# Sixteen pad writes issued before, not after, the placement of the last attention maxima

## The reference

```python
xn = layernorm(x)
x = x + L0_attn(xn) + L0_ffn(xn)
xn = layernorm(x)
x = x + L1_attn(xn) + L1_ffn(xn)

# L1_ffn, for xt of shape (T, 128)
topk_logits, topk_idx = top_k(xt @ Wg.T, 2)
gates = zeros.at[rows, topk_idx].add(softmax(topk_logits))
h = gelu(einsum('th,ehi->tei', xt, W1) + b1)
y = einsum('te,teh->th', gates, einsum('tei,eih->teh', h, W2) + b2)
```

## Time and profile before

| what | us |
|---|---|
| median of 3 runs | 1333.94 (1332.34 to 1334.08) |
| the profiled execution | 1332.34 |
| its span in the profile | 1330.6 |
| PE busy | 1235.0 (93%) |
| DVE busy | 809.0 (61%) |
| ACT busy | 714.4 (54%) |
| POOL busy | 587.5 (44%) |

### The profile page before, as it was taken

The page is one execution under the profiler, slowest core; times in us unless marked ns, Lnnn a source line. Parts: engine busy times, 40 slices in busy tenths (PEclk is TensorE's granted clock), DMA queues, the critical chain, the costliest instruction groups (busy, mean ns, idle before and its releaser), DMA issues. The chain is left out here.

```text
span 1330.6 us, 26366 instructions
## 1 busy us (share of the span) xinstructions
PE 1235.0 (93%) x9090; PEld 870.0 (65%) x9090; DVE 809.0 (61%) x3359; ACT 714.4 (54%) x1532; POOL 587.5 (44%) x776
## 2 busy tenths in 40 slices
PE   5988999999999999999999999999999965899997
PEld 2555577657765776577656765676566644489997
DVE  4064487638863885378637863786468557656563
ACT  2365267625772577247734773477436720657675
POOL 7133254415441544244325442444245434358787
PEclk9999999999999999999999999999999976899999
DMA  7603320333023402340234023301440006134453
GB/s 222 163 3 108 112 65 7 99 108 82 9 89 87 114 9 88 88 110 12 81 96 110 13 81 96 107 14 58 119 105 16 3 28 227 35 61 67 57 68 45
DMA packets 84085, 101.84 MB, mean 77 GB/s; under 512 B 12537, under 2 KB 45217, under 8 KB 83873
## 3 DMA queue, kind: packets, MB, share of 16 engines
q1 hardware_dynamic: 65360, 82.22, 22.5%
q0 software_dynamic: 13792, 9.54, 4.9%
q10 hardware_dynamic: 4800, 8.39, 1.9%
HBM read 55.44 MB, written 46.37 MB: 77 GB/s over the span
## 5 line engine op out<-in xcount | busy, mean ns | idle before, releaser
L1000 ACT ACTIVATE probs<-bank 128x512 f32<-128x512 f32 (+2 forms) x896 | 442.3, 580 | 252.5 <-PE bank L614 246.6
L614 PE MATMUL bank<-K,Q 128*128 128x192 f32 (+4 forms) x1024 | 244.6, 319 | 9.2 <-issue 8.5
L1170 POOL TENSOR_SCALAR_AFFINE_SELECT probs<-probs 128x384 f32<-128x384 f32 x256 | 127.2, 519 | 276.5 <-ACT probs L1000 275.5
L614 PE MATMUL bank<-Q,K 128*128 128x192 f32 (+4 forms) x1024 | 215.6, 318 | 1.3 <-DMA Q<-mrow_c 1.3
L671 PE MATMUL heads<-probs,V 128*9 128x192 f32 (+4 forms) x3072 | 196.4, 397 | 13.9 <-DVE probs L1407 5.6
L614 PEld LDWEIGHTS bank<-K,Q 128*128 128x128 f32 x1024 | 172.3, 196 | 36.4 <-issue 22.5
L614 PEld LDWEIGHTS bank<-Q,K 128*128 128x128 f32 x1024 | 150.3, 192 | 31.3 <-issue 19.0
L671 PEld LDWEIGHTS heads<-probs,V 128*9 128x9 f32 x3072 | 75.8, 91 | 125.9 <-issue 83.4
L990 ACT ACTIVATE probs<-bank,sh_s 128x512 f32<-128x512 f32 x64 | 44.0, 688 | 210.1 <-PE bank L607 199.3
L614 PE MATMUL bank<-QM,K 128*128 128x512 f32 (+3 forms) x512 | 139.8, 337 | 11.2 <-DVE mx_s L1355 6.2
L1220 POOL DMA_INDIRECT out<-h1T_s x78 | 124.0, 1590 | 42.5 <-issue 26.2
(11 more groups left out here) (188 smaller groups left out, 2040.2 us busy)
## 6 DMA issues: line engine op xcount, KB each, us to landing
Q<-slots_of_q SPq DMA_DIRECT2D x15, 1024.0 KB, 10.1
K<-slots_of_k SPq DMA_DIRECT2D x60, 192.0 KB
QM<-slots_of_qm SPq DMA_DIRECT2D x8, 1024.0 KB, 8.4
slots_of_q<-Q SPq DMA_DIRECT2D x24, 256.0 KB, 3.0
slots_of_k<-QM SPq DMA_DIRECT2D x24, 256.0 KB, 3.9
slots_of_qm<-Q SPq DMA_DIRECT2D x24, 256.0 KB, 4.1
slots_of_k<-Q SPq DMA_DIRECT2D x24, 256.0 KB, 3.0
slots_of_q<-Q ACTq DMA_DIRECT2D x24, 256.0 KB, 4.8
```

The lines of the kernel that those rows point to most:

```text
L614: mm = pe.matmul(to[:, at:at + right.shape[1]], left, right, start=True, stop=True, skip_group_check=True)
L1000: return act.activation(to, bank, func, scale=scale, bias=bias).then_inc(taken_sem(run, unit), 1)
L1170: pool.affine_select(out=three, in_=three, compare_op=ALU.is_ge, fill=0.0, base=0, pattern=[[0, 3], [1, P]], channel_multiplier=-1)
```

## The change

In SP's function `tail`, the call of `place_causal` moves from ahead of the pad writes to behind them. Its 8 transfers and its two waits, the two waits ahead of the pads and the 16 pad writes are the same as before.

```diff
             def tail():
-                place_causal(("tail", NB))
                 sp.wait_ge(S["pads_counted"], 1)
                 sp.wait_ge(S["routing_set"], ROUTING)
                 for n in range(K2 * E):
                     row = sp.value_load(pad_at[0:1, n:n + 1], min_val=0, max_val=K2 * REGION - P)
                     sp.dma_start(sorted_rows[bass.ds(row, P), :], pad_row[:, :]).then_inc(S["pads_sent"], 16)
+                place_causal(("tail", NB))
```

## The result

The changed kernel takes 1348.2 us (median of 4 runs, 1345.8 to 1349.5), the kernel before 1334.0 us in the same comparison. The ratio is 1.0103, with a 95% interval of 1.0083 to 1.0125: 14.2 us slower. The forecast was 1334.5 us and no measurable change, with a range up to 1339.0. What was measured is the time of rival C, 1347.8 us.

What follows compares the result with a forecast made beforehand. The tail's attention, waiting on DVE, was taken to bound the kernel. SP late 0.58 us, plus 0 each for queue, second half and tiles, gave +0.6 us on 1333.94: 1334.5 us, range 1332.0 to 1339.0.

Steps and rivals of the forecast that it cites:

- rival C: SP's pads cannot be issued until the expert loads' backlog drains; placement 13.9 us late, 1347.8 us; chance 0.10.
- What bounds the kernel: In the tail, a later placement delays the maxima and everything after nearly one for one; an earlier one gives at most 0.21 us.
- The cost of a pad, 1.128 us: On SP, each pad takes 0.33 us of issue and 0.80 us of register load; the block of 16 takes 17.25 us.
- SP being late: SP finishes the 16 pads after the first maxima are ready, so the placement starts 0.58 us later.
- The queue term, 0: In SP's queue, the pads' backlog is gone before the placement's last transfer; 0 to 1.8 us, taken as 0.
- The second half of the placement and the tile part, 0: SP's second placement is unchanged; tile loads and store go earlier but nobody waits for them; 0 us each.
- B, slower register loads: SP's register loads for pads slow beside full DMA engines; 5.0 us at half as much again, 1338.9 us; chance 0.14.
- D, faster: In the tile part, earlier tile loads and store gain at most 1.2 us, less the 0.6: 1333.3 us; chance 0.06.

Runs made afterwards that it cites:

- experiment 1: The changed kernel with the 4 MB of expert loads issued behind the tail's transfers; 1332.1 us against 1331.0 for the kernel before, ratio 1.0011.
- experiment 9: The changed kernel run once more, unaltered; 1344.9 us in one run, the kernel before 1331.7.
- experiment 3: The changed kernel with the second expert matrix loaded in 1024 rows of 2 KB, not 4096 of 512 bytes; 1339.4 us in one run, before 1331.0.
- experiment 7: The kernel before with the 16 pads issued from ACT's queue ahead of its tail stage; 1330.1 us against 1331.4, ratio 0.9997.
- experiment 2: The kernel before with one more 65 KB write, to a fixed DRAM address, behind SP's expert loads; 1330.5 us in one run, before 1331.0.
- experiment 4: The changed kernel with only the first expert matrix ahead of the pads, the second behind the tail's transfers; 1329.1 us in one run, before 1331.4.
- 5: The changed kernel with the expert loads issued between the pads and the placement; 1347.9 us in one run, before 1331.4.
- 8: The changed kernel with 8 pads ahead of the placement and 8 behind it; 1335.9 us against 1331.4 for the kernel before, ratio 1.0038.
- experiment 6: The changed kernel with the expert loads issued from ACT's queue at the start of its tail; 1338.4 us against 1331.0 for the kernel before, ratio 1.0059.

## Why the prediction was wrong, step by step

**What bounds the kernel: right.** A late placement went through one for one: 16.0 us more waiting on PE for a placement 16.1 us late, and 15.5 us more span.

**The cost of a pad, 1.128 us: right where nothing is held.** The block was 17.17 us in experiment 1 and, without its hold, 17.22 us in 9. The gap ahead of the first pad was 1109.49 − 1108.16 = 1.33 us, taken as 1.38.

**The step that failed is the dismissal of rival C:** "What accepted 2 MB within 1.08 us at the height of the backlog should accept 65 KB after it." A short issue of the second matrix only showed that SP had handed it over, not that its 4096 rows had gone on. The next issue waits until most of them have, 11.54 us in the profile after and 11.32 us again in experiment 9. I compared rates (407 GB/s out, 58 GB/s in) where the state at the start counts: the queue was full. The sum had 0.58 us for SP being late. With the hold it is 0.58 + 11.0 = 11.6 us for an execution like that of experiment 9 (placed 12.4 us late, from 1125.30 to 1137.71) and 0.58 + 11.2 + 2.9 = 14.7 us for the first profile (16.1 us late). The 0.8 and 1.4 us that are left come about with a term that the sum took as fixed: the maxima were ready 18.06 us after SP had issued the expert loads before, but 17.2 us after it in experiment 9 and 16.6 us in the first profile, where PE stood idle 5.8 and 5.1 us ahead of its first maxima and not 6.9. C had the right mechanism, but its 13.9 us meeting the 14.2 us is partly luck. It had SP idle until the engines drained, with a register load still to come, and the pad in fact was let go while 0.34 MB were left, with its register load done; so experiment 9 is only 12.4 us late, and the first profile's 2.9 us are in no term of C's.

The Trainium skill ("Perfetto Trace Analysis", DMA Instruction — HWDGE), which I had set beside C, has an issue last until all its descriptors are generated, against a buffer that can be full. The trace agrees in that an issue can be long while its own data are small (0.33 and 11.54 us for the same 65 KB). It doesn't bear out the rule for the load itself: the 2 MB of 512-byte rows were issued in 0.84 us, and the transfer behind them carries the wait. In the same section the Trainium skill has a lock wait, until the descriptor generator is free, ahead of that inside the same row. Whether the 11.54 us are that wait or the generating, no row here tells.

**The queue term, 0: not put to the test by the change itself,** since the placement no longer followed a backlog. In experiment 1, right behind 16 pads, PE starts 4.06 us after the first placement's start (1121.84 to 1125.90), and before the change 4.19 us. By then only the last pad or two were under way in experiment 1, since each landed within 3.6 us of its issue, so pads that go out as fast as they are issued do not delay it. A placement behind a real backlog of pads was not tried.

**The second half of the placement and the tile part, 0: right** (148.45 us from first to last add, before 148.71).

**B, slower register loads: refuted.** Their median is 0.268 us in the profile after and 0.271 us in experiment 3, where many more of them run beside full engines. **D, faster: not seen.** The interval of experiment 7, 0.9980 to 1.0014, could not tell its 0.6 us from nothing, but the traces speak against it: POOL's first add starts 5.57 us after PE's first turn before the change, 5.58 us after the change and 5.57 us in experiment 7, although the store is issued 1.0 us behind that turn in the first and 0.2 us ahead of it in the other two. The margin is thin. In experiment 2 the store came 3.1 us behind the turn, and there it did release POOL, 6.35 us after the turn.

## What to carry to other kernels

A transfer that is issued in under a microsecond can still block the next one on its queue for most of the time that its rows take to go out: 7.4 to 13.9 us behind 4 MB here, and nothing behind 2 MB in 1024 rows. Before anything is moved to a place behind a large load, ask how long that engine has really been able to issue there: an idle stretch in the row of a queue is only free if nothing large was issued ahead of it. A small transfer that somebody waits for belongs ahead of the large load, or on a queue that has none; on another queue the large load must still not run beside a fetch that is due.

## What the runs showed of the hardware

What came behind the expert loads on SP's queue, by run:

| rows ahead of it (expert loads) | longest issue behind them, us |
|---|---|
| none (experiment 1) | 0.40 |
| 1024 of 2 KB (4) | 0.39 |
| 2048 of 2 KB (3) | 7.41 |
| 1024 of 2 KB, 4096 of 512 B (after, 2, 5, 8, 9) | 11.54, 13.86, 10.93, 11.89, 11.32 |
| the same 4 MB in SP's queue, pads in ACT's (7) | 0.39 |
| none, but keys, queries and pads in SP's queue beside 4 MB from ACT's (6) | 3.20 |

So 1024 rows of 2 KB pass, and the same again does not. What stood unsent in SP's queue, counted by its packets in the traces:

- Bytes are not the measure. In experiment 6 a pad is held with 1.1 MB unsent, in experiment 4 the first pads pass with 2.3 MB and more, and in experiment 3 the pad is let go with 2.4 MB left.
- The size of the rows matters. The same 2 MB hold the pad for 11.54 us in rows of 512 bytes and for 7.41 us in rows of 2 KB. The trace does not show why, since the engines' packets are of 2 KB in both. Of the changed kernel, 1119 to 1121 us:

```profile
DMA packets 373, 0.76 MB, mean 382 GB/s; under 512 B 0, under 2 KB 0, under 8 KB 373
```

- No fixed number of rows fits. Behind the 512-byte rows the issue was let go with 0.34, 0.13, 0.65, 0.24 and 0.37 MB left (after, 2, 5, 8, 9), which is 260 to 1,260 rows. In experiment 3 it was 1,150 rows of 2 KB, while experiment 4 passes with about 1,320 rows unsent and experiment 6 holds at about 1,180.

So the rows matter and not the bytes alone, but the limit itself stays open. It may be one for each DMA engine and not for the queue as a whole, or a rule that the transfer before must be handed over to the last row; no run separates the two.
